# A graph layer's 833 gather-and-sum steps: written out one by one, or as a loop of 49 turns with two steps to a PSUM bank

## The reference

```python
def _gcn_layer(x, src, dst, norm, W, b, num_nodes):      # called twice
    xw = x @ W
    msg = xw[src] * norm[:, None]
    out = jax.ops.segment_sum(msg, dst, num_segments=num_nodes)
    return out + b

xn = _layernorm(x)
x = x + gnn(xn, edge_index, ...) + linear_attention(xn, ...)   # gnn: elu(gcn), twice
x = x + moe_ffn(_layernorm(x), ...)                            # 8 experts, top 2
```

## Time and profile before

| | us |
|---|---|
| median of 3 runs | 3330.49 (3329.08 to 3338.45) |
| the profiled execution | 3338.05 |
| its span, first to last instruction | 3336.2 |
| layer 0, first gather to last add | 1167.8 |
| layer 1, first step to last add | 1157.0 |
| everything else | 1011.4 |

### The profile page before, as it was taken

One profiled execution on the slowest core, in us unless ns is written; L12 is line 12 of the kernel. 1 busy time (PEld: TensorE's weight loads), 2 busy tenths in 40 slices (PEclk: granted clock), 3 DMA queues, 4 the chain that ended last, 5 costly groups with the idle time before them and its releaser, 6 DMA issues. The chain is left out here.

```text
span 3336.2 us, 45400 instructions
## 1 busy us (share of the span) xinstructions
PE 2378.8 (71%) x10847; PEld 1766.3 (53%) x10847; DVE 1766.5 (53%) x4443; ACT 619.5 (19%) x1318; POOL 1965.2 (59%) x2107
## 2 busy tenths in 40 slices
PE   3367677767677767465666656666669399999998
PEld 2244444444444446243444434444448199999997
DVE  6144444444444456254445545555557766777765
ACT  2000000000000005010001101111116344444443
POOL 1666666666666653666666666666633045555554
PEclk9677877877888788676777777777789599999999
DMA  6333333333333322444444444444422465555551
GB/s 170 114 92 92 90 90 92 92 90 91 88 91 90 89 71 90 116 142 143 141 137 148 145 142 138 146 147 146 145 74 67 146 202 147 146 148 149 148 148 21
DMA packets 177904, 397.27 MB, mean 119 GB/s; under 512 B 42393, under 2 KB 96570, under 8 KB 169514
## 3 DMA queue, kind: packets, MB, share of 16 engines
q0 software_dynamic: 96800, 233.29, 26.9%
q1 hardware_dynamic: 50926, 103.38, 8.6%
q10 hardware_dynamic: 30012, 58.67, 5.1%
HBM read 322.87 MB, written 75.01 MB: 119 GB/s over the span
## 5 line engine op out<-in xcount | busy, mean ns | idle before, releaser
L644 POOL DMA_INDIRECT rows<-rows_layer,srcs x1564 | 1538.4, 984 | 767.6 <-issue 384.3
L705 PE MATMUL l_bank<-rows,sel 128*128 x3332 | 1190.7, 489 | 636.6 <-issue 228.4
L695 DVE TENSOR_TENSOR acc<-acc,l_bank 128x256 f32 x1666 | 699.1, 420 | 1237.2 <-remote 515.9
L705 PEld LDWEIGHTS l_bank<-rows,sel 128*128 128x128 f32 x3332 | 705.3, 236 | 997.2 <-issue 468.8
L1637 PE MATMUL ps_y<-whl,hhi 128*128 128x512 f32 x896 | 320.8, 398 | 0.0
L1593 POOL DMA_INDIRECT out<-ys,g_sum x112 | 182.2, 1627 | 198.1 <-DVE ys L1549 172.9
L673 DVE TENSOR_TENSOR sel<-iota_n,dloc 128x512 f32<-128x512 f32 x418 | 286.7, 686 | 20.1 <-issue 20.1
L1508 ACT ACTIVATE hr<-ffn_bank,vec 128x256 f32<-128x256 f32 x448 | 212.7, 475 | 375.9 <-PE ffn_bank L1449 335.4
L1447 PE MATMUL ffn_bank<-xh,whl 128*128 128x256 f32 x896 | 252.2, 281 | 2.4 <-DVE xl L1523 2.4
L1448 PE MATMUL ffn_bank<-xl,whl 128*128 128x256 f32 x896 | 252.2, 281 | 0.0
L1449 PE MATMUL ffn_bank<-xh,whl 128*128 128x256 f32 x896 | 252.0, 281 | 0.0
(11 more groups left out here) (273 smaller groups left out, 2240.8 us busy)
## 6 DMA issues: line engine op xcount, KB each, us to landing
whl<-w_hi SPq DMA_DIRECT2D x32, 1024.0 KB
whl<-w_lo SPq DMA_DIRECT2D x32, 1024.0 KB
rows<-rows_layer,srcs POOLq DMA_INDIRECT x1564
w_qkv<-wide ACTq DMA_DIRECT2D x49, 335.0 KB
w_hi<-whi ACTq DMA_DIRECT2D x49, 335.0 KB
w_lo<-wlo ACTq DMA_DIRECT2D x49, 335.0 KB
rows_layer<-acc SPq DMA_DIRECT2D x25, 256.0 KB, 2.1
rows_x<-acc SPq DMA_DIRECT2D x7, 910.0 KB
```

The source lines that it names most:

```text
L644: pool.indirect_dma_start(rows[:, (n + 1) % ROWS, :], None, table[layer], bass.IndirectOffsetOnAxis(ap=srcs[:, n:n + 1], axis=0)).then_inc ...
L695: v.tensor_tensor(to, to, step_bank(s), ALU.add).wait_op(sem(f"summed{layer}"), s + 1, "sem-ge").then_inc(sem(f"added{layer}"), 1)
L705: t.matmul(step_bank(s), sel[:, s % SELS, :], rows_flat[:, bass.ds(slot * D, D)], start=True, stop=True).wait_op(sem(f"here{layer}"), t.to ...
```

## The change

TensorE's and VectorE's parts of a layer become: turn 0 written out, a loop `Fori(1, 48)` over turns 1 to 47 with 16 steps in its body, turn 48 written out, and the last 49 steps written out. ScalarE's part is a loop over the blocks likewise. GpSimd's and SyncE's parts stay written out as they were.

Step numbers in a loop are `first + k`, with `first` in a register. So the words of the table are loaded, and the columns of `dloc` for a select are found, by an address from a register, and each threshold that was a constant is computed into a register. The places of `sel` must come out the same each turn, so there are 16 of them.

Banks: steps 2j and 2j+1 share bank j % 4, one in each half (`step_bank`). TensorE waits for `added` at even steps alone, until both sums of the bank eight steps back are added. VectorE's add of an even step waits until both sums of the bank are there; the odd one waits for the add before it alone. So four banks hold eight sums, and the selects run 10 to 13 steps ahead.

```diff
-ROWS, SELS, FOUR = 32, 12, 4
+ROWS, SELS, FOUR = 32, 16, 4
-AHEAD = 6
 PSB = 4
+SUMS = 2 * PSB
+AHEAD = SUMS + 2
...
         def step_bank(s):
-            return step_ps[s % PSB][:, 0:D]
+            return step_ps[s // 2 % PSB][:, s % 2 * D:(s % 2 + 1) * D]
...
+        def number(eng, n):
+            return n if isinstance(n, int) else eng.to_reg(eng.snap(n))
+
-        def step_add(v, layer, s, block):
-            if s > 0:
-                v.wait_ge(sem(f"added{layer}"), s)
+        def step_add(v, layer, first, k, block, whole):
             to = acc[:, bass.ds(block, D)]
-            v.tensor_tensor(to, to, step_bank(s), ALU.add).wait_op(sem(f"summed{layer}"), s + 1, "sem-ge"
-                                                                   ).then_inc(sem(f"added{layer}"), 1)
+            if k % 2 == 0:
+                until = number(v, first + (k + 2 if whole else k + 1))
+                ins = v.tensor_tensor(to, to, step_bank(k), ALU.add).wait_op(sem(f"summed{layer}"), until, "sem-ge")
+            else:
+                until = number(v, first + k)
+                ins = v.tensor_tensor(to, to, step_bank(k), ALU.add).wait_op(sem(f"added{layer}"), until, "sem-ge")
+            ins.then_inc(sem(f"added{layer}"), 1)
...
-        def step_sum(t, layer, s, here):
+        def step_sum(t, layer, first, k, here):
             slot = t.snap(here & (ROWS - 1))
             t.to_reg(slot)
-            if s < PSB:
-                t.wait_ge(sem(f"selected{layer}"), s // FOUR + 1)
-            else:
-                t.wait_ge(sem(f"added{layer}"), s - PSB + 1)
+            if isinstance(first, int) and first + k < SUMS:
+                t.wait_ge(sem(f"selected{layer}"), k // FOUR + 1)
+            elif k % 2 == 0:
+                t.wait_ge(sem(f"added{layer}"), first + (k - SUMS + 2))
...
+        def tensor_turn(t, layer, first, many, between):
+
+            tiles = tiles_of(first, min(LOADED, many))
+            for k in range(many):
+                step_sum(t, layer, first, k, tiles[k])
+                if k % LOADED == 1 and k + LOADED - 1 < many:
+                    tiles.extend(tiles_of(first + (k + LOADED - 1), min(LOADED, many - k - LOADED + 1)))
+                between(k)
+
+        def turns(eng, body, layer, between):
+
+            body(eng, layer, 0, TURN, lambda k: between(0, k, True, False))
+            with eng.Fori(1, NT - 1) as i:
+                body(eng, layer, eng.snap(i * TURN), TURN, lambda k: between(i, k, False, False))
+            body(eng, layer, (NT - 1) * TURN, TURN, lambda k: between(NT - 1, k, False, True))
+            body(eng, layer, NT * TURN, STEPS - NT * TURN, lambda k: None)
...
-                    for i in range(NT):
-                        one(i, i == 0)
+                    one(0, True)
+                    with a.Fori(1, NT) as i:
+                        one(i, False)
```

More of the change, by code:

```diff
@@ L708, in vector_steps @@
-        def vector_steps(v, layer, between):
[L710 to L720, removed]
@@ new lines, in step_sum, with vector_turn @@
+            t.matmul(step_bank(k), sel[:, k % SELS, :], rows_flat[:, bass.ds(slot * D, D)], start=True, stop=True
+                     ).wait_op(sem(f"here{layer}"), t.to_reg(here), "sem-ge").then_inc(sem(f"summed{layer}"), 1)
+        def vector_turn(v, layer, first, many, between):
+            blocks = blocks_of(first, min(LOADED, many))
+            for k in range(many):
+                if k % LOADED == 1 and k + LOADED - 1 < many:
+                    blocks.extend(blocks_of(first + (k + LOADED - 1), min(LOADED, many - k - LOADED + 1)))
+                if k % FOUR == 2 and (not isinstance(first, int) or first + k + AHEAD < STEPS):
+                    four_selects(v, layer, first, k + AHEAD)
+                if k % 2 == 0 and not (isinstance(first, int) and first + k == 0):
+                    v.wait_ge(sem(f"added{layer}"), first + k)
+                step_add(v, layer, first, k, blocks[k], k + 1 < many)
+                between(k)
@@ L732, in dense @@
+        def vector_steps(v, layer, between):
+            for s in range(0, AHEAD + 2, FOUR):
+                four_selects(v, layer, 0, s)
+            turns(v, vector_turn, layer, between)
+        def tensor_steps(t, layer, between):
+            turns(t, tensor_turn, layer, between)
         def dense(ap):
@@ L1042, in one @@
                         a.activation(mixb[:, :], ps_o[:, 0:D], ACT.Copy).then_inc(sem("a_mix"), 1)
-                    for i in range(NT):
-                        one(i, i == 0)
+                    one(0, True, False)
+                    with a.Fori(1, NT - 1) as i:
+                        one(i, False, False)
+                    one(NT - 1, False, True)
                     a.wait_ge(sem("w_lo"), NT)
@@ L1051, in _, with between @@
                 def _(v):
-                    def between(i, k):
-                        is_first = i == 0
-                        if k == 0 and i == NT - 1:
+                    def between(i, k, is_first, is_last):
+                        if k == 0 and is_last:
                             v.wait_ge(sem("a_xadd"), NT - 1)
```

48 lines of the change are left out of this document (19 added, 29 removed).

## The result

The change made the kernel slower: a median of 3369.48 us (3365.91 to 3374.93, 4 runs) beside 3333.5 us (3329.08 to 3338.45, 4 runs) for the kernel before on the same chip, a ratio of 1.0112 with an interval of 1.0091 to 1.0133. The forecast of 3196 us had the wrong sign.

A forecast was written before the change was run, and what follows sets the result against it. It took the late hand-over between TensorE and VectorE, holding up GpSimd's gathers, as the bound: 3338 - 173 (banks) + 39 (register work) = 3204 us profiled, median 3196 us, own range 3110 to 3290, with rivals 3030 to 3390.

The forecast's parts named there:

- Eight sums in four banks: Both graph layers: TensorE six to eight steps ahead instead of four halves GpSimd's 346.2 us of slot waits, saving 173 us.
- below 100: Sign of a right forecast: TensorE's waits for an add, 204.9 us before, fall below 100 us.
- nothing, if TensorE stands in other waits at those times: Lower bound of the banks' gain in the graph layers; the upper bound was all 346.2 us.
- 0.17 us a gather: Mid-layer gather spacing of 1.456 us less 1.284 us, taken as GpSimd's waiting for slots that SyncE frees.
- the wait moves: Rival, chance 0.10: in the layers TensorE stands at once-a-turn waits for VectorE and ScalarE instead; 3320 to 3345 us.
- Register work, +39 us, bounds 0 to 85: VectorE's sequencer in 94 turns: 0.9 us each, 85 us, mostly hidden behind gathers; 39 us taken, TensorE's included.
- Adds in pairs: VectorE's even add waits about 1 us for one more sum; costs nothing while TensorE is ahead.
- Table loads: VectorE and TensorE: still four a turn, number and exposed time stay except where two come close; counted as nothing.
- Instruction fetches, 0: Most of TensorE's and VectorE's instruction fetch traffic goes; 0.2% of the DMA engines' time, worth nothing as bandwidth.
- the rival on them: Rival, chance 0.06: an engine fetches instructions at each branch back, 94 times 0.8 us; exposed 75 us, 3405 us.
- the gathers become the bound: Rival, chance 0.20: GpSimd's waits vanish, each layer takes about 1010 us; 3025 to 3060 us in all.
- longer chain: Rival, chance 0.16: added instructions on VectorE's and TensorE's sequencers count, 174 us at most, half exposed; 3417 us.

The follow-up runs named there:

- The banks alone: Kernel before, all steps written out, but two sums to a bank, eight ahead, waits in pairs; 0.9976 in a late series, 1.0030, 1.0029 and 1.0034 on time.
- late condition: Series where SyncE's list waits for TensorE's sums; the kernel before takes about 3330 to 3360 us.
- on time: Series where SyncE's list waits for the gathers to land; the kernel before takes about 3030 us.
- The loops alone: The change's loops with one sum to a bank, four ahead as before; against the kernel before 1.0022 late, 1.0023, 1.0031 and 1.0050 on time.
- Moving the dense work: Changed kernel, layer 0's projections after step 7 not 3, VectorE's part after 12 not 8, keys by values after 15 not 13; late 3336.34 us, 1.0007 against before.
- with both: The changed kernel, with loops and two sums to a bank, against the kernel before; late 1.0112 and 1.008, on time 1.0028.
- The changed kernel with the later dense work and slots freed 8 tiles behind: Changed kernel, layer 0's dense work later in the turn, SyncE freeing slots 8 tiles behind instead of 16; on time 1.0003 and 1.0002 against before.

## Why the prediction was wrong

*Eight sums in four banks, -173 us: this step failed.* "Each pause of GpSimd then pays for twice the steps, and so about half as many are needed." The banks alone gave 7 us in the late condition (3349.51 beside 3356.87) and cost 8 to 9 on time. GpSimd's waits for slots were 329.9 us with the banks alone, and 346.2 (362 waits) became 399.1 (361 waits) with the whole change; its pauses over 2 us were 57 and 63 in two traces of the kernel before, 52 with the banks alone, 83 and 77 in two of the kernel after. Twice the lead did not halve them.

The way of the wait stands in the kernel and in the earlier trace rows, which I had read: the waits end with SyncE's L666, and that instruction waits for `summed`, which TensorE raises, not for `added`. The banks can act on it only through TensorE's own waits for an add. These fell nearly as predicted (from 204.9 to 108.9 us, in a second trace 79.9, where I had said below 100), and GpSimd's waits did not follow. The late news itself is left as it was: SyncE's waits for it are 678.8 + 480.6 us before and 719.5 + 515.6 after. My bound "nothing, if TensorE stands in other waits at those times" was nearest; I took the middle because TensorE's wait for a bank "has the same size" as GpSimd's wait, which says nothing on cause. Why TensorE's news is late stays open.

The size that I halved was misread too. Each of the 362 waits holds the 0.30 us that lie between any two gathers, some 109 us in all; so about 240 of the 346.2 us could be had at most, and half of that is 120. My own 0.17 us a gather says much the same: 269 us for 1564 gathers.

*The rival "the wait moves"* had the mechanism at 0.10, and not its price. What I named as its sign, TensorE's idle time ahead of the transposes, projections and attention matmuls, is what came (projections 37.0 to 243.7 us). But its price was put at 3320 to 3345 us, and the same pace that I read as its protection (687 gathers in 1000 us) fell to 662 in layer 0. Moving the dense work took the loss back, so the layer and the placement are shown. Why layer 0 loses time in the kernel after and not with the banks alone, which have the stand too, is argued, not shown. A turn of layer 0 is a ring there: the projections, the steps to the turn's head, the transposes, their late semaphore, ScalarE's copy, the projections again. In the mean of the layer a turn takes 23.44 us with both (second trace) and 22.84 with the banks alone. The projections account for most of this difference: 231.8 and 207.3 us busy in 49 turns, 0.50 us a turn. They run slow behind a stand: in the first trace of the kernel after, 37 turns have a long stand ahead of them, 6.5 us in the mean, and there the granted clock is 0.55 and the eight matmuls take 5.1 us; in the 9 turns without one it is 0.97, and they take 2.9 us. The Trainium skill (TensorE: Matmul & The Clock Gate, Part 1: The HAM clock gate) ties the 1.2 GHz level to a TensorE that has been idle; the window shown above, 5.49 us at 0.50 behind a stand of 5.66 us, agrees. The traces with both and with the banks alone are of different series, so these 0.50 us are no more than a pointer.

*Register work, +39 us, bounds 0 to 85.* VectorE's sequencer has 458 x 53, 1128 x 57, 376 x 57, 282 x 86, 94 x 98 and 80 x 46 ns in the layers, 147 us, and with some smaller ones and the branches 165 us, where it had 1666 x 46, 77 us: 88 us more, as the 85 us that I had worked out. The loops alone cost 0.2%, 6 us, late, and 0.2 to 0.5%, 7 to 11 us, on time. The size of the work was right; what was exposed of it was less than the 39 us, unless the rival of the last section holds and the loops cost more where the kernel before takes 3333 us.

*Adds in pairs, 0*: VectorE does 10 adds from 110 to 155 us where it did 7, so the pair is no brake there; it was not tried apart from the banks. *Table loads*: still 947 and 987 ns in the median, and 418 on each engine. *Instruction fetches, 0, and the rival on them*: 21 packets instead of 68 and 59 instead of 98. With 94 turns on each of VectorE and TensorE a fetch at each branch back would have made more packets, not fewer. The rule of the Trainium skill (Runtime: NRT & Kernel Launch, Instruction fetch mechanics) did not come into force with bodies of 16 steps, and the rival is false.

*The rival "the gathers become the bound"*, 3025 to 3060 us by 782 x 1.284 us a layer, describes the on-time condition, and holds there for every kernel with gathers, the kernel before too (3030 to 3033 us). The arithmetic was right. The 3333 us go with the late semaphores and the 3030 us with those on time in every trace, and no part of this change touches them.

*The rival "longer chain"* gave the right sign, at 3417 us. In their own late series the loops alone cost 0.2%, so it was small there; whether it is in the series of the result stays open, as said above.

No version beats both kernels clearly. The banks alone, with the steps written out, are 0.24% faster than before in the one late series that they met, and 0.3% slower on time. The changed kernel with the later dense work and slots freed 8 tiles behind equals the kernel before on time.

## What to carry to other kernels

Before a wait is priced by a remedy, follow the semaphore that ends it to the engine that raises it: a remedy that is not on that path only moves idle time elsewhere. A deeper buffer lets an engine run ahead until its next fixed hand-over; try that hand-over at a later place, and judge it by the layer's time, for here the idle time only moved on while the loss went. Take the gap that any two issues have out of a wait before you call it a gain to be had. And run the kernel before in several series before a gain is worked out from one trace: here its own bound changed by 9% between series.

## What the runs showed of the hardware

The same kernel takes 3030 us in some series and 3333 or 3357 to 3361 in others, each on another chip where the chip is known, and most runs of a series lie within 0.3% of its median. In the late series a semaphore instruction of SyncE that otherwise always takes 17 ns takes up to 1.4 us (ns, min/median/max, after late, then after on time, `here` of both layers):

```profile
L662 SPq EVENT_SEMAPHORE  x1564: 1/17/1396, 98.1 to 2503.3; - x196
```
```profile
L662 SPq EVENT_SEMAPHORE  x1564: 17/17/17, 98.0 to 2185.6; - x196
```

In the stretch from 110 to 155 us of the late trace of the kernel before the median of SyncE's semaphore instructions is 0.70 us, while the gathers are issued at full pace; on time they take 17 ns beside the same gathers. So the gathers alone do not make the delay, as my prediction would have it; something that differs between the series must be there too. What that is stays open.
